# Cross-network tower on one core: the second layer's four partial sums are ended by one strided tensor_reduce in place of two additions

## What is computed

```python
x0 = xk = e                      # e: [1024, 39, 16], the looked-up rows
for W in (f0, f1, f2):           # W: [39*g, 128]; g is 39 in the first layer, then 128
    z = jnp.einsum('bfd,bgd->bfgd', x0, xk).reshape(b, 39 * g, d)
    cur = jnp.einsum('bpd,pm->bmd', z, W)
    outs.append(cur)
    xk = cur
result = jnp.sum(jnp.concatenate(outs, axis=1), axis=-1)
h = relu(concat([result, dense_ctx]) @ W_top1 + b_top1)
h = relu(h @ W_top2 + b_top2)
y = h @ W_top3
```

## Time and profile before

| | |
|---|---|
| median of three runs | 1332.29 us (1331.56 to 1333.27) |
| the profiled execution, its own time | 1330.08 us |
| its span | 1328.3 us |
| mean granted TensorE clock over the span | 0.992 of full speed |
| busy share: TensorE matmul, weight load, VectorE, ScalarE, GpSimd | 96%, 76%, 87%, 69%, 79% |

### The profile page before, as it was taken

How to read it: one execution, slowest core, us unless ns; L and a number is a source line. 1 busy time by engine, 2 the same in 40 slices (tenths; PEclk the granted TensorE clock), 3 DMA queues, 4 the chain that set the end, 5 groups by cost and what they waited for, 6 DMA issues and landing times. The chain is left out here.

```text
span 1328.3 us, 21624 instructions
## 1 busy us (share of the span) xinstructions
PE 1276.6 (96%) x5983; PEld 1015.4 (76%) x5983; DVE 1155.5 (87%) x3210; ACT 915.7 (69%) x3053; POOL 1050.0 (79%) x743
## 2 busy tenths in 40 slices
PE   4799999999999999999999999999999999999998
PEld 2487777887778777887778877788777877788787
DVE  3499999699988999789996999969999799988983
ACT  2377776577766777677775777757776677767783
POOL 7588888688886888779887788968888688884661
PEclk9799999999999999999999999999999999999999
DMA  7732333322333332223333033331233322223000
GB/s 192 163 58 53 61 64 65 62 38 47 53 62 62 64 58 43 47 52 62 66 64 59 10 64 66 64 62 15 57 64 65 62 54 44 45 57 62 1 3 1
DMA packets 129421, 76.08 MB, mean 57 GB/s; under 512 B 90792, under 2 KB 98201, under 8 KB 129301
## 3 DMA queue, kind: packets, MB, share of 16 engines
q1 hardware_dynamic: 119061, 72.07, 26.6%
q0 software_dynamic: 10240, 2.64, 2.3%
HBM read 68.16 MB, written 3.87 MB: 54 GB/s over the span
## 5 line engine op out<-in xcount | busy, mean ns | idle before, releaser
L392 ACT ACTIVATE parts<-pieces,x_cols 128x128 f32<-128x128 f32 x2560 | 718.1, 377 | 166.1 <-PE pieces L688 164.0
L526 DVE SCALAR_TENSOR_TENSOR parts<-pieces,x_cols,parts 128x128 f32<-128x128 f32 x2432 | 679.4, 340 | 113.2 <-PE pieces L688 92.0
L686 PE MATMUL pieces<-w_hi,cur_hi 128*128 128x512 f32 (+1 forms) x1280 | 548.1, 428 | 22.4 <-DVE parts L526 22.2
L688 PE MATMUL pieces<-w_hi,cur_lo 128*128 128x512 f32 (+1 forms) x1280 | 498.6, 390 | 0.0
L687 PE MATMUL pieces<-w_lo,cur_hi 128*128 128x512 f32 (+1 forms) x1280 | 498.4, 389 | 0.0
L340 POOL TENSOR_TENSOR parts<-parts 128x1024 f32<-128x1024 f32 x127 | 320.3, 2522 | 140.0 <-DVE parts L526 136.8
L331 POOL DMA_INDIRECT emb<-in_table,rows x320 | 342.2, 1069 | 80.8 <-issue 62.1
L686 PEld LDWEIGHTS pieces<-w_hi,cur_hi 128*128 128x128 f32 x1280 | 241.5, 189 | 93.5 <-DVE parts L526 43.8
L411 ACT ACTIVATE pairs_hi<-pairs 117x512 fp32r<-117x512 f32 (+1 forms) x224 | 141.9, 634 | 202.2 <-DVE pairs L536 192.2
L688 PEld LDWEIGHTS pieces<-w_hi,cur_lo 128*128 128x128 f32 x1280 | 240.9, 188 | 51.5
L687 PEld LDWEIGHTS pieces<-w_lo,cur_hi 128*128 128x128 f32 x1280 | 242.0, 189 | 47.7
(11 more groups left out here) (66 smaller groups left out, 596.4 us busy)
## 6 DMA issues: line engine op xcount, KB each, us to landing
partners<-x_wide SPq DMA_DIRECT2D x62, 546.0 KB
partners<-x_wide SPq DMA_DIRECT2D x31, 468.0 KB
x_rep<-x_wide SPq DMA_DIRECT2D x96, 78.0 KB
emb<-in_table,rows POOLq DMA_INDIRECT x320
x_diag<-x_cols SPq DMA_DIRECT2D x256, 10.0 KB
x_wide<-emb SPq DMA_DIRECT2D x32, 80.0 KB
x_wide<-emb SPq DMA_DIRECT2D x32, 32.0 KB
wt<-in_wt SPq DMA_DIRECT2D x1, 1024.0 KB
```

The lines of the kernel that those rows point to most:

```text
L392: last = nc.scalar.activation(parts[n % 2][:, 4 * i + r, :], src[:, r * H:(r + 1) * H], ACT.Copy, scale=x_cols[n // 4][:, n % 4, f:f + 1])
L526: nc.vector.scalar_tensor_tensor(acc, src[:, r * H:(r + 1) * H], x_cols[n // 4][:, n % 4, f:f + 1], acc, ALU.mult, ALU.add).then_inc(acc_d ...
L686: nc.tensor.matmul(dst[:, 0:width], hi[:, cols], w1_hi[:, ws], start=True, stop=False)
L688: nc.tensor.matmul(dst[:, 0:width], lo[:, cols], w1_hi[:, ws], start=False, stop=True).then_inc(l2d_ready if q in D_PIECES else l2a_ready, 1)
```

## The change

Between piece 7 and piece 8 of a block VectorE ran two additions, L580 over 256 columns and L586 over 128 columns, with the semaphore `halved` between them. Now there is one tensor_reduce in piece 8. It reads the 512 columns of `tails` in the order m, j: for each of the 128 outputs the four partial sums, which lie 128 numbers (512 bytes) apart. What L580 waited for (`tree_done`) the reduce waits for, and it keeps L586's wait for `g_ready`.

```diff
-            def halve_tails(u, n):
-                g, v = u * BLOCKS + n, tails[n % 2]
-                dve.wait_ge(tree_done, (g + 1) * TREE)
-                nc.vector.tensor_tensor(v[:, 0:2], v[:, 0:2], v[:, 2:4], ALU.add).then_inc(halved, 1)
-
             def finish_cur2(u, n):
                 g, v = u * BLOCKS + n, tails[n % 2]
                 wait(dve, g_ready, g - 1)
-                dve.wait_ge(halved, g + 1)
-                nc.vector.tensor_tensor(cur2[n % 2][:], v[:, 0], v[:, 1], ALU.add).then_inc(cur2_ready, 1)
+                dve.wait_ge(tree_done, (g + 1) * TREE)
+                nc.vector.tensor_reduce(cur2[n % 2][:], v[:].rearrange("p j m -> p m j"), AX.X, ALU.add
+                                        ).then_inc(cur2_ready, 1)
...
-                        if q in (Q_HALVE, Q_FINISH):
-                            step = halve_tails if q == Q_HALVE else finish_cur2
+                        if q == Q_FINISH:
                             if n >= 2:
-                                step(u, n - 2)
+                                finish_cur2(u, n - 2)
                             elif not first:
-                                step(u - 1, BLOCKS + n - 2)
+                                finish_cur2(u - 1, BLOCKS + n - 2)
```

More of the change, by code:

```diff
@@ L73 @@
 G_LAG = 3
-Q_HALVE, Q_FINISH = 7, 8
+Q_FINISH = 8
 FIELDS = 4
@@ L192, in cin_kernel @@
         tree_done = sem("tree_done")
-        halved = sem("halved")
         cur2_ready = sem("cur2_ready")
@@ L632, in _ @@
             over_quads(dve, quad)
-            halve_tails(QUADS - 1, BLOCKS - 2)
             finish_cur2(QUADS - 1, BLOCKS - 2)
             add_last_parts()
-            halve_tails(QUADS - 1, BLOCKS - 1)
             finish_cur2(QUADS - 1, BLOCKS - 1)
```

## The result

The change makes the kernel slower: 1361.24 us against 1332.39 us, 28.9 us more, ratio 1.0216 (95% interval 1.0201 to 1.023). The profiled execution took 1361.92 us, its span is 1360.1 us. That is 1.2 us above the range and 27.7 above the forecast.

What follows compares the result with a forecast made beforehand. TensorE paces the 43.2 us tiles, VectorE with GpSimd's L340 tiles 2 and 3. 22 block 2 passages x 0.06 us, less 0.13, gave +1.2 us: 1333.5 us against the runs' median, range 1330 to 1360.

Steps and rivals of the forecast that it cites:

- What bounds the kernel: TensorE paces the 43.2 us tiles; in tiles 2 and 3 VectorE has next to nothing to spare, its position set by L340.
- the wait of block 2: GpSimd's L340 waits 0.90 to 0.93 us for VectorE 29 times; seven in tile 0 left out, 22 counted.
- The price of the reduce: VectorE's new tensor_reduce: 0.60 us start to start, like L561 reading PSUM; upper bound 1.13 us.
- the prediction's own scheme: Extra VectorE time paid in full at 22 block 2 passages; in blocks 0 and 1 of 24 tiles only beyond the slack.
- the slack: In blocks 0 and 1, 0.35 us by which VectorE can be later before GpSimd's L340 is delayed.
- The moved pairs instruction: VectorE's pairs instruction starts 0.34 us earlier, so ScalarE's L411 and then L552 or TensorE's L668 can start earlier.
- the cover of the blocks 0 and 1: GpSimd's gathers hide the reduce's 0.06 us there; without them it would cost 2.9 us more.
- The strided read: Rival: the strided SBUF read costs VectorE a second column time, 0.53 us more per reduce; 1357 us, chance 0.33 with lesser penalties.
- the earlier pairs: Rival: pairs starting 0.34 us earlier gain once in each of 22 tiles, 7.5 us; 1326 us, chance 0.09.
- the late `cur2`: Rival: `cur2` ready 0.06 us later lengthens TensorE's 27 weight-load waits, 1.6 us more; 1335.1 us, chance 0.08.
- The signs in the profile: Reduce about 0.68 us if right, over 0.75 for the rival; tiles 2 and 3 over 1 us longer if strided read is dear.

Runs made afterwards that it cites:

- the reduce in piece 1 of block 2: Against the kernel before: only in block 2 of each tile, one strided reduce in piece 1 replaces the two additions; 1321.83 us, ratio 0.9929.
- the row form: Against the changed kernel: same reduce in the same place, reading four neighbours side by side, so other quadruples are summed; 1343.31 us, ratio 1.0082 to the kernel before.
- the move without any reduce: Against the kernel before: its two additions side by side in piece 8, so the pairs instruction moves up; 1347.81 us, ratio 1.0116.

## Why the prediction was wrong

*What bounds the kernel* held in the main. The tile of 43.2 us did not change, the tiles 2 and 3 took the larger part of the loss, VectorE's held instruction and GpSimd's addition set each other's time, and the reduce in piece 1 of block 2, built on that reading alone, came out in its range. It did not hold in tile 0 of the quads 1 to 7. There the prediction let TensorE take over the pace, and left the wait of block 2 out of its sum; the stretch grew by 0.84 us all the same, 0.54 of it between the row form and the strided form, which differ in the price of the reduce alone.

*The price of the reduce* is the step that failed first: "so I take 0.60 and keep 1.13 for the range". Measured is 0.99 from start to start. ScalarE reading PSUM was a poor neighbour for VectorE reading SBUF: there 160 bytes between neighbours cost nothing, here 16 bytes already cost 0.4 us. With 0.06 + 0.39 = 0.45 in place of 0.06 the prediction's own scheme gives 22 x 0.39 + 48 x (0.45 - 0.35) = 13.4 us between the strided and the row form; the runs show 17.9. Two things that the scheme lacks can be read. In the blocks 0 and 1 the slack was not used up, for L339 still starts right behind a gather that has itself become longer. Instead L339 takes 2.53 us in block 1 of the changed kernel and 2.42 in the row form, since VectorE's next pairs instruction, coming later, runs into its start. And the stretch of tile 0 that takes 43.59 us in the changed kernel takes 43.05 in the row form, where the scheme has 2 x 0.10 for the blocks 0 and 1 and nothing for block 2:

```profile
521.88:564.93 43.05, 41.73 (x216) 34.17 (x215) 37.23 (x97) 27.27 (x92) 37.94 (x29) 1.00 0.27 51
```

How the 17.9 us divide between these was not worked out.

*The moved pairs instruction* is the step that was left out: "the pairs instruction starts 0.34 us earlier" was weighed as a gain alone, and GpSimd's gathers were named as the cover of the blocks 0 and 1 without asking whether they stay as long. They grew by 0.26 us in each. By the same scheme that is 24 x 2 x 0.26 = 12.5 us; the row form, in which the reduce costs no more than L561, lost 10.9 us, and the move without any reduce 15.4, of which 22 x 0.19 = 4 are its own longer additions.

*The rivals.* The strided read was the right one, with 0.33. Its 1357 us lay near by two errors that offset each other: it took 0.53 for a step of 0.39 and knew nothing of the collision. No kernel with the earlier pairs alone was faster (1347.81 us for the move). TensorE's weight loads for `make_g` did wait more for the late `cur2` (33.9 us in 76 waits against 6.7 in 27); the tiles 2 and 3 show that this is not what made them longer: VectorE stands still there for 37.70 - 37.44 = 0.26 and 38.10 - 37.85 = 0.25 us, less than before (0.73 and 0.45), and with the reduce in piece 7 these waits are down to 6.4 us in 18, in a kernel that takes 1360.14 us. Whether they add something in tile 0 was not taken apart.

*The signs in the profile* named beforehand were the right ones: a reduce over 0.75 us, and tiles 2 and 3 longer by over 1 us. That the other tiles would stay unchanged was wrong for tile 0.

## What to carry to other kernels

Before a reduce over a strided view, look at the distance of the neighbours in bytes, and take the price from a row of the same engine and the same memory, or call it unknown and forecast between the bounds. When an instruction is removed, look at what moves into its place and which other engine it meets there: here a pairs instruction that cost VectorE nothing more held up GpSimd. An expensive instruction with one SBUF input is free where VectorE would be held by GpSimd anyway; that place, not a lower count of instructions, made the faster kernel.

## What the runs showed of the hardware that I had not expected

- A tensor_reduce of 512 fp32 columns from SBUF takes 672 to 676 ns with neighbours 4 or 8 bytes apart and 1048 to 1115 ns from 16 bytes on.
- A gather that GpSimd starts while VectorE is in an instruction with two SBUF inputs ends some 0.83 us behind that instruction: it took 0.97, 1.05, 1.23 and 1.31 us with 0.13, 0.23, 0.40 and 0.50 us of it left. One that VectorE starts later, during the gather, leaves it at 0.95. The Trainium skill (SBUF — State Buffer, Who interferes with whom) says that such an instruction contends with a GpSimd instruction that reads SBUF, and infers that it does not stall descriptor generation. The held additions here agree with the first; the gather's late start and its 0.95 us beside a later instruction do not contradict the second. What in the gather is held at its start is not shown.
- A tensor_reduce from SBUF is not held by GpSimd's addition (1.08 us right through one of 2.44), as the same section says.
- Two dependent additions on VectorE can be held one after the other by two GpSimd additions (1.65 and 1.17 us in place of 0.41 and 0.28).
